# Cross-attention denominators of the second sequence: sums of four steps instead of two, and POOL's sums one after another by its own signal

## The reference, cut to what matters

```python
q = (x1 @ wq.T).reshape(b, n, HEADS, HEAD_DIM).transpose(0, 2, 1, 3)
k = (x2 @ wk.T).reshape(b, m, HEADS, HEAD_DIM).transpose(0, 2, 1, 3)
v = (x2 @ wv.T).reshape(b, m, HEADS, HEAD_DIM).transpose(0, 2, 1, 3)
dots = jnp.einsum('bhnd,bhmd->bhnm', q, k) * SCALE
attn = jax.nn.softmax(dots, axis=-1)
out = jnp.einsum('bhnm,bhmd->bhnd', attn, v)
```

## Time and profile before

| | us |
|---|---|
| median of 3 runs (1865.8 to 1867.45) | 1866.66 |
| the profiled execution's own time | 1869.96 |
| span of that profile | 1867.9 |
| PE busy (of the span) | 1843.9 (99%) |
| DVE busy | 1256.4 (67%) |
| ACT busy | 878.9 (47%) |
| POOL busy | 850.0 (46%) |
| L2286, POOL's sums of two steps, 464 instructions | 584.8 |
| L1448, PE's sets, 744 records | 98.7 |
| L1780, DVE's transposes of visits, 78 instructions | 55.6 |

### The profile page before, as it was taken

The page is one execution under the profiler, slowest core; times in us unless marked ns, Lnnn a source line. Parts: engine busy times, 40 slices in busy tenths (PEclk is TensorE's granted clock), DMA queues, the critical chain, the costliest instruction groups (busy, mean ns, idle before and its releaser), DMA issues.

```text
span 1867.9 us, 27863 instructions
## 1 busy us (share of the span) xinstructions
PE 1843.9 (99%) x10488; PEld 1290.6 (69%) x10488; DVE 1256.4 (67%) x2339; ACT 878.9 (47%) x1587; POOL 850.0 (46%) x822
## 2 busy tenths in 40 slices
PE   9999999999999999999999999999999999999998
PEld 7786688788655555555555554554469998899986
DVE  6675574278787888888798799778554444344457
ACT  4322323322665666666465465457624443344433
POOL 4002201100598999998677577676122223222232
PEclk9999999999999999999999999999999999999999
DMA  8003535684767586858554443451244454534544
GB/s 289 24 1 118 186 103 178 199 243 144 170 139 168 130 202 130 176 112 178 109 135 114 103 118 87 112 115 63 79 148 127 132 142 107 141 91 131 145 111 155
DMA packets 124502, 250.19 MB, mean 134 GB/s; under 512 B 11312, under 2 KB 29504, under 8 KB 119680
## 3 DMA queue, kind: packets, MB, share of 16 engines
q1 hardware_dynamic: 109696, 187.56, 34.3%
q0 software_dynamic: 14672, 60.85, 16.0%
HBM read 148.46 MB, written 62.42 MB: 113 GB/s over the span
## 4 chain that ended last, share of the span: by engine, by line
PE 86%; DVE 9%; DMA 2%; issue 1%; POOL 1%; SPq 0%; ACT 0%; DVEq 0%; POOLq 0%; ACTq 0%
PE banks L1225 35%; PE banks L1540 12%; PE banks L1413 11%; PE banks L1424 11%; PE banks L1394 10%; DVE max L1758 5%; PE banks L1448 4%; PE banks L1231 2%; DMA raw<-in_x_t 1%; DVE den_t L1780 1%; PE banks L1325 1%; DMA k_half<-in_xwk_t 0%; DMA k_stack<-k_parts 0%; POOL x_nat L2297 0%; DVE hot_row L1936 0%
## 5 line engine op out<-in xcount | busy, mean ns | idle before, releaser
L2286 POOL TENSOR_TENSOR probs<-probs,probs 128x512 f32<-128x512 f32 x464 | 584.8, 1305 | 194.1 <-PE banks L1424 193.1
L2164 ACT ACTIVATE probs<-banks 128x512 f32<-128x512 f32 x1024 | 517.6, 626 | 286.9 <-PE banks L1413 286.4
L1758 DVE TENSOR_REDUCE max<-banks 128x1 f32<-128x512 f32 x1024 | 626.2, 680 | 37.4 <-PE banks L1394 37.0
L1413 PE MATMUL banks<-q_stack,k_stack 98*128 98x512 f32 x1024 | 403.3, 407 | 0.1
L1394 PE MATMUL banks<-k_stack,q_stack 98*128 98x512 f32 x1024 | 400.1, 398 | 1.4 <-DVE den_t L1780 1.1
L1413 PEld LDWEIGHTS banks<-q_stack,k_stack 98*128 98x128 f32 x1024 | 191.0, 187 | 151.7 <-issue 101.1
L1424 PE MATMUL banks<-probs,v_grp 128*32 128x512 f32 x2048 | 252.3, 605 | 0.0
L1394 PEld LDWEIGHTS banks<-k_stack,q_stack 98*128 98x128 f32 x1024 | 192.6, 188 | 48.5 <-DVE max L1758 13.5
L2344 POOL DMA_INDIRECT y_rows<-eo,tok x35 | 69.8, 1994 | 172.3 <-DVE eo L1991 116.2
L1424 PEld LDWEIGHTS banks<-probs,v_grp 128*32 128x32 f32 x2048 | 60.3, 110 | 118.3 <-issue 112.0
L1978 DVE TENSOR_TENSOR hid_lo<-hid,hid_hi 128x640 fp32r<-128x640 f32 x64 | 52.8, 824 | 126.3 <-ACT hid_hi L2233 126.3
(11 more groups left out here) (273 smaller groups left out, 2795.8 us busy)
## 6 DMA issues: line engine op xcount, KB each, us to landing
k_stack<-k_parts SPq DMA_DIRECT2D x144, 256.0 KB, 5.4
probs<-probs POOLq DMA_DIRECT2D x36, 1024.0 KB, 10.1
w_raw<-in_L_ffn_w SPq DMA_DIRECT2D x16, 2048.0 KB, 8.4
q_stack<-q_parts SPq DMA_DIRECT2D x48, 256.0 KB
v_grp<-v_rows SPq DMA_DIRECT2D x48, 256.0 KB, 3.5
raw<-in_ctx_t SPq DMA_DIRECT2D x8, 1024.0 KB, 6.6
k_parts<-out_hi SPq DMA_DIRECT2D x32, 256.0 KB, 2.5
k_parts<-out_lo SPq DMA_DIRECT2D x32, 256.0 KB, 3.2
```

Source lines behind the costliest of these rows:

```text
L1413: nc.tensor.matmul(out, keys_of(t)[0:STK + SHIFT, j, tile_of(s)], queries_of(t)[:, j, :], start=True, stop=True).then_inc(scored.sem, 1)
L1758: V.reduce_max(max4[:, tiles_of(t), :, :][:, k, j, mc:mc + 1], bank(bank_of["max", t, mc, k, j]), AX.X) \
L2164: S.activation(probs_of(t, s)[:, j, :], bank(bank_of["score", t, s, j]), ACT.Exp, scale=SCALE) \
L2286: G.tensor_tensor(a[:, j, :], a[:, j, :], b[:, j, :], ALU.add).then_inc(pair_added.sem, 1)
```

## The change

`LATER_FOURS` had 5 quarters of the second sequence. It now has 24: all quarters of turns 8 to 13 but the last quarter of turn 11, and the first quarter of turn 14. Quarter (11, 2), the last in fours before one in twos, is put into `LAST_BEFORE_PLAIN`. And in the second sequence the second, third and fourth of POOL's four sums of a block wait until the one before them has signalled that it is done. What is summed stays the same.

```diff
-LAST_BEFORE_PLAIN = {(2 * NG - 1, 2)}
-
-LATER_FOURS = {(8, 0), (8, 1), (10, 1), (13, 0), (13, 1)}
+LAST_BEFORE_PLAIN = {(2 * NG - 1, 2), (3 * NG - 1, 2)}
+
+LATER_FOURS = {(t, q) for t in range(2 * NG, 4 * NG - 2) for q in range(4)} - {(3 * NG - 1, 3)} | {(4 * NG - 2, 0)}
...
                 pool.wait_ge(*num_summed[t, s - 1])
+                if groups[turns[t][0]][0] and j:
+                    pool.wait_ge(*pair_added[t, s, j - 1])
                 G.tensor_tensor(a[:, j, :], a[:, j, :], b[:, j, :], ALU.add).then_inc(pair_added.sem, 1)
```

## The result

The changed kernel takes **1882.3 us** (median of 4 runs, 1880.82 to 1885.76), the kernel before 1867.06 on the same chip (4 runs, 1865.8 to 1869.21). The ratio is 1.0089, 95% interval 1.0072 to 1.0105: slower by 15 us, where I forecast 14 us faster. The profiled execution took 1882.95 us.

The account below looks back on a forecast made before the run. PE was taken to set the pace, with the chain through DVE where it has side work. Sets removed, 15.0 us, less 1.0 for block 115, gave 14.0 us: 1866.66 to 1852.7 us, range 1847 to 1861.

Parts of the forecast that it names:

- (3): POOL's issue of the 19 added transfers, 0.87 us each, fits into its idle time in each block.
- (4): 156 own-signal waits between POOL's sums: 0.11 us each, 0.3 per block, cost 0; cover gone above 0.19 each.
- rival B: Gaps between POOL's sums let DVE's held routing instructions pass: 4 us more gain, 1848.7 us; chance 0.12.
- (1): PE's sets in blocks 69 to 117 of the second sequence: 19 fewer, gaining 15.0 us.
- (2): 19 added 1 MB transfers in the second sequence: DMA share 68%, nobody waits, cost 0.
- Rival E: Transfers land late, so ACT then PE stand still once per quarter: slower, 1876.7 us at one microsecond each; chance 0.10.
- (5): Block 115, double visit (last of turn 13, first of turn 14): DVE's second transpose waits for POOL; 1.0 us, bounds 0 to 3.

Follow-up runs that it names:

- run 14: As run 1, but in three blocks (steps 12 and 13 of turns 9, 11, 13) POOL's four sums take 2 of 512 columns: 1865.95 us, 0.9998.
- run 3: The kernel before with own-signal waits between POOL's sums in the blocks of the first sequence: 1874.56 us, 1.0047.
- run 2: The kernel before with the three own-signal waits in each block of the second sequence, its five quarters in fours kept: 1873.17 us, 1.0032.
- run 4: The changed kernel with the last quarter of turn 13 and the first of turn 14 in twos, so no double visit: 1881.62 us, 1.0074.
- run 5: As run 1, with own-signal waits only in the block of steps 12 and 13 of turns 9, 11 and 13: 1868.19 us, 1.0018.
- run 1: The changed kernel without the own-signal waits, all 24 quarters in fours: 1879.79 us, 1.0067.
- run 8: The kernel before with the first three quarters of turn 9 in fours as well, no own-signal waits: 1866.87 us, 1.0004.
- run 6: As run 5, with the last quarter of turn 13 and the first of turn 14 in twos: 1873.1 us, 1.0027.
- run 7: Eleven quarters in fours (first three of turns 8, 10, 12, first two of 13) against five in the kernel before, no waits: 1867.6 us, 1.0008.
- run 10: As run 9, with the last quarter of turn 13 and the first of turn 14 in twos: 1868.01 us, 0.9999.
- run 13: As run 12, with the last quarter of turn 13 and the first of turn 14 in twos: 1870.45 us, 1.0012.
- run 9: As run 1, with POOL's first sum in 24 blocks waiting for the maximum behind DVE's side work: 1869.73 us, 1.0016.
- run 12: As run 1, with POOL's first sum waiting for DVE's maximum behind side work in three blocks only (turns 9, 11, 13): 1874.66 us, 1.0044.

## Why the prediction was wrong

The forecast was 14 us faster and the result is 15 us slower. The step that failed is what stood under all others unsaid: that DVE's operations keep their durations when blocks move, a cost put at nothing in steps (3) and (4), where POOL's queue was only asked whether it has the time. It was 12.5 us slower instead of 15 faster with the fours alone, and 12.9 of it hang on three rows of POOL's sums (run 14). I read in the earlier trace rows that a small operation stands still for 1.2 us beside a sum, and used it only as a gain in rival B. I never asked where the side work would lie against POOL's sums once a block loses 0.86 us on PE, and never asked what a stop of PE does to its clock.

- **(1) Sets removed, 15.0 us.** The count was right (19 sets, 592 records). The price was too high: in run 14, which has no long hold, turns 8 to 13 are 1.3, 1.3, 1.3, 1.2, 2.0 and -0.1 us shorter than before, 7.1 in sum. Turns are cut here at the end of the numerators, so the set of a turn's last block falls into the next turn; counted so, my list of blocks has 1.7, 3.9, 1.5, 4.2, 1.9 and 0.9, together 14.0. Turns 8, 10 and 12 came nearly as listed. 5.6 of the missing 7 us are in turns 9 and 11, with routing on DVE, and 1.0 in turn 13. In turns 9 and 11 PE stands for 1.0 and 1.6 us more than before, and DVE's short holds take 1.1 and 2.4 us more: the same mechanism, in small. The rest of these two turns stays open.
- **(2) Transfers, cost 0.** Right. They land in a median of 10.4 us, the DMA share from 888 to 1300 us is 0.68 as worked out, and no engine waits for one in that stretch. Rival E had the right sign for the wrong reason.
- **(3) POOL's issue, covered.** POOL does have the time. But wherever a long hold stands, copy, divisions and issue had brought POOL to its sums without a stop, at the very moment of DVE's side work. I had counted the time that these take, not where they put the sums.
- **(4) Own-signal waits, 0.11 each, cost 0.** They cost 0.18 to 0.19 us each instead of 0.11, 0.55 a block, just at the 0.19 that I had named as the end of the cover. Where POOL is tight they set the pace (run 3), and in the second sequence 6 us are lost although POOL idles 1.69 us in the block shown: its sums last until DVE's side work begins (run 2). In the changed kernel they also did good, since 5.22 us of hold became 2.00 and 1.11. There the two effects nearly cancel: 1882.3 with the waits, 1879.8 without, with overlapping intervals.
- **(5) Block 115, 1.0 us.** DVE's second transpose did wait for POOL, 3.50 us. Turn 14 takes 2.5 us more than without the double visit (the changed kernel against run 4), although it has two sets fewer: PE stands for 2.9 us more, and the clock is at 0.97 instead of 1.00. That is within my bounds of 0 to 3, but the total didn't change when the double visit was taken out.
- **Rival B** named the right mechanism, and I gave it the wrong use: a pause in POOL's row lets DVE in, worth 9 to 12 us in three blocks (run 5), but only against holds that the fours had made.

The account of run 1 by what the profiles show: 12.5 us slower than before, and 12.9 to 13.8 go with the three rows of sums. Turns 9 to 14 are 17.5 us longer in run 1 than in run 14. PE's idle time makes 14.6 us of it, nearly all in the three stops of 5.3, 4.9 and 4.9 us, and its busy time 2.9: 3.7 more in turns 9, 11 and 13, where the matmuls behind the stops are slow, and 0.8 less in turn 12, where run 14 has the lower clock. Turn 15 gives 3.3 us back, at a clock of 1.00 against 0.94, which leaves the 14.0 between the spans. What is left is level with the kernel before: turns 8 to 13 gain 7.1 us, turn 14 loses 3.4, and the medians (1865.95 and 1866.58) differ by less than the profiled spans do, that of before being one of its longer executions.

Open: why POOL's row sometimes gives way after one sum and sometimes after four. In the three long holds POOL had come to its sums from other work with no idle time, in the hold of 1.25 us at 951.57 us in run 1 it had waited 2.19 us for PE. In run 8 a pause of 0.16 us ahead of the row was enough: the operation that met its first sum was held for 1.26 us. That is a pattern, not a proof. Open too is what brings the clock down in turn 12: it stood at 0.92 in the profiles of runs 6, 7 and 10, at 0.94 in the changed kernel and run 13, at 0.97 in runs 4, 9 and 14, and at 1.00 in runs 1, 5 and 12.

No version was faster than the kernel before by more than the noise.

## What to carry to other kernels

When a change shortens blocks, list the small operations of other engines that will now fall beside a long one on an engine with which they exclude each other, here DVE's operations from SBUF to SBUF beside POOL's sums. Price a hold by the whole row of the long operations, not by one, and add what TensorE loses by its clock behind the stop (here 0.6 to 1.7 us for each of three stops of 5 us). When work is moved rather than removed, count it where it lands, with the cuts between stages laid as in the profile. Queued work right ahead of such a row is a warning even if the engine has time to spare. A wait that is "covered" on its own engine still moves the end of what it stretches, so look at who starts there.

## What the runs showed of the hardware

- One small operation of DVE (128 x 8 or 128 x 4, 0.16 to 0.17 us alone) stood for 5.10 to 5.22 us behind four sums of POOL, in three places of run 1; with own-signal waits between the sums 1.1 to 2.1 us, with the sums cut short 0.24 (run 14). Operations with two inputs in SBUF, CAST, COPY and TENSOR_SCALAR were all held at some place; BATCH_NORM_STATS, MAX8, the maxima and the transposes, both from PSUM, never were in any of the profiles.
- An own-signal wait on POOL between two sums of 1.29 us costs 0.18 to 0.19 us (run 2, four sums in 5.59 instead of 5.02 us).
- TensorE's granted clock fell to 0.50 after a stop of 5.3 us (run 1) and, in one profile, after stops of 1.0 us at the longest (run 8), and stayed there for some 6 us both times. The same turn 15 took 54.76 us at a mean clock of 1.00 and 57.90 at 0.94.
- Executions of one kernel then differ by 10 us and more, and their mean clock goes along: in run 5 1865.31 us at 0.998 and 1879.33 at 0.989, in run 8 1863.54 at 0.998 and 1878.59 at 0.993. How much of such a difference the clock makes, and how much the stops ahead of its falls, no run separates.
